# A fused adaLN block: who opens and who adds the eight partial groups of a feed-forward step

## The chip, the cores and the metric

The kernel runs on one core of a Trainium2 chip. The metric is the device time of one execution in microseconds.

## What is computed

The reference is one transformer-like block over 4096 tokens of width 512. Its first half (layer norm, a cumulative attention, a gated projection) is not touched. The second half is the feed-forward:

```python
h = _layernorm(x) * (1 + cb) + sb
gate_up = einsum('bsh,oh->bso', h, w_gu)      # w_gu: 2816 x 512, 4-bit values times scales
gate, up = gate_up[..., :1408], gate_up[..., 1408:]
y = einsum('bsi,hi->bsh', silu(gate) * up, w_down)
x = x + gb * (y / sqrt(mean(y * y) + 1e-6))
```

The scales of `w_gu` hold for groups of 128 input channels, so a product over 512 inputs is four group sums, each scaled by itself.

## The kernel before

The tokens are worked through in NB = 8 blocks of T = 512, features on the partitions. The function `ffn` is the second stage. A block has I_T = 11 steps j, one for each 128 hidden units. In a step TensorE computes GROUPS = 8 groups m: 0 to 3 are the four input groups of the gate, 4 to 7 those of the up half. Each is two matmuls (high and low part of the input) into one PSUM bank of `EV`. After every second group TensorE adds three matmuls of the down projection of step j - 2 (`down`), into four other banks. So a step has 28 matmuls of 128x512.

The banks: `ev_bank(j, m)` is m % 4, but m % 3 in the steps 2 to 5 (`R_STEPS`), where the fourth bank is `R`, used for the sums over channels. `before(j, m)` finds the group that had the bank last, and TensorE waits for its taker.

A group is taken out of its bank with its scale (`take`) into `A`, a float32 buffer with three slots of four tiles: the even groups by ScalarE, which opens a tile (L1445), the odd ones by VectorE, which scales and adds to the tile (L1621). So a step has four tiles, each the sum of two groups. GpSimd's `half` (L1525) adds tile 1 to tile 0 (gate) and tile 3 to tile 2 (up). ScalarE's `silu` (L1455) works on tile 0. `hidden` multiplies tile 0 by tile 2: on GpSimd (L1531) at the steps in `POOL_STEPS`, at the others on VectorE (L1628). ScalarE's `high` (L1451) rounds the product to float16 in `HH`, GpSimd's `low` (L1535) forms the rest, and both feed `down` (L1335) two steps later. ScalarE's first take of a step waits until `low` has left the slot (`slot_free`).

Each engine's order is written out by hand. Beside the takes, `beside` puts one instruction of the next block's norm and of the last block's output at fixed places; place 4j + i is the pair of groups i of step j. On VectorE these are: centring at places 9 to 12 (L1567), quarter reciprocals of the variance's root at 22 to 25 (L1573), the scale at 26 to 29 (L1585), the low part of the input (low_n, L1591) at 30 to 33, quarter reciprocals for the output at 34 to 37, its norm (L1598) at 38 to 41 and the result (L1613) at 40 to 43. GpSimd has nine additions at places 1 to 19 (L1505, L1514). The reductions on TensorE stand at places 8 (mean, L1313, which also waits for all takes of steps 0 and 1 in `sums_left`), 17 and 21.

Of the kernel before, what the change touches and what calls it, by code (L numbers as in the profile page):

```python
# [15 lines left out]
ALU = mybir.AluOpType  # L16
# [1122 lines left out]
def ffn(nc, v):  # L1139
# [7 lines left out]
    with ExitStack() as ctx:  # L1147
# [22 lines left out]
        EV = bank[0:4]  # L1170
# [10 lines left out]
        R_STEPS = range(2, 6)  # L1181

        def ev_bank(j, m):
            return m % (3 if j in R_STEPS else 4)
# [53 lines left out]

        POOL_STEPS = (1, 2, *range(5, I_T))

# [58 lines left out]
        def _(pe):  # L1299
# [6 lines left out]
            def sums_left(b):  # L1306

                pe.wait_ge(by_dve, DT * (I_T * b + R_STEPS.start))
                pe.wait_ge(by_act, DT * (I_T * b + R_STEPS.start))

# [30 lines left out]
            def iteration(b, s, prev, nxt):  # L1341
# [3 lines left out]
                for j in range(I_T):  # L1345
                    for m in range(GROUPS):
# [13 lines left out]
                        if last is None:  # L1360
                            n = b + 1 if nxt else b
                            bank_free(n, n, b if prev else 0)
                        elif not (j == 0 and last[0] and first(b)):

                            back, k = last
                            pe.wait_ge((by_act, by_dve)[k % 2], DT * (I_T * b + j - back) + k // 2 + 1)
                        which, g = m // DT, m % DT
# [17 lines left out]
            bank_free(NB - 1, NB - 1, NB - 1)  # L1385
            pe.wait_ge(by_dve, DT * I_T * NB)
            pe.wait_ge(by_act, DT * I_T * NB)
            for c in range(DT):
# [5 lines left out]
        def _(act):  # L1394
# [43 lines left out]
            def take(b, j, m):  # L1438
# [3 lines left out]
                if m == 0:  # L1442
                    slot_free(act, HH_low, b, j)
                t = which * I_T + j
                nc.scalar.activation(A[:, slot(j), 2 * which + g // 2, :], EV[ev_bank(j, m)][:], ACT.Copy,  # L1445
                                     scale=gu_s[:, t, g:g + 1]).then_inc(by_act, 1)
# [6 lines left out]
            def silu(b, j):  # L1453
                act.wait_ge(halves, 2 * (I_T * b + j) + 1)
                nc.scalar.activation(A[:, slot(j), 0, :], A[:, slot(j), 0, :], ACT.Silu).then_inc(gate_silu, 1)  # L1455
# [17 lines left out]
            def iteration(b, s, prev, nxt):  # L1473
                for j in range(I_T):
                    for m in range(0, GROUPS, 2):
                        beside(b, s, DT * j + m // 2, prev, nxt)
                        if m == GROUPS - 2:
                            if j:
                                high(b, j - 1)
                            elif prev:  # L1480
                                high(b - 1, I_T - 1)
                        take(b, j, m)
                    silu(b, j)
# [13 lines left out]
        def _(pool):  # L1497
# [23 lines left out]

            def half(b, j, which):
                pool.wait_ge(by_dve, DT * (I_T * b + j) + 2 * which + 2)
                a = A[:, slot(j), 2 * which, :]
                nc.gpsimd.tensor_tensor(a, a, A[:, slot(j), 2 * which + 1, :], ALU.add).then_inc(halves, 1)  # L1525

            def hidden(b, j):
                pool.wait_ge(gate_silu, I_T * b + j + 1)
                pool.wait_ge(halves, 2 * (I_T * b + j) + 2)
                a = A[:, slot(j), 0, :]  # L1530
# [14 lines left out]
            def iteration(b, s, prev, nxt):  # L1545
                for j in range(I_T):
                    if j in POOL_STEPS:
                        hidden(b, j - 1)
                    for i in range(DT):
                        if i == DT - 2:  # L1550
                            half(b, j, 0)
                        if i == DT - 1:
# [4 lines left out]
                        beside(b, DT * j + i, prev, nxt)  # L1557
                    half(b, j, 1)

# [4 lines left out]
        def _(dve):  # L1564
# [50 lines left out]
            def take(b, j, m):  # L1615

                which, g = m // DT, m % DT
                dve.wait_ge(group_done, GROUPS * (I_T * b + j) + m + 1)
                dve.wait_ge(by_act, DT * (I_T * b + j) + m // 2 + 1)
                a = A[:, slot(j), 2 * which + g // 2, :]  # L1620
                nc.vector.scalar_tensor_tensor(a, EV[ev_bank(j, m)][:], gu_s[:, which * I_T + j, g:g + 1], a,  # L1621
                                               ALU.mult, ALU.add).then_inc(by_dve, 1)

            def hidden(b, j):
                dve.wait_ge(gate_silu, I_T * b + j + 1)
                dve.wait_ge(halves, 2 * (I_T * b + j) + 2)
                a = A[:, slot(j), 0, :]
# [15 lines left out]
            def iteration(b, s, prev, nxt):  # L1643
                for j in range(I_T):
                    for m in range(1, GROUPS, 2):
                        beside(b, s, DT * j + m // 2, prev, nxt)
                        take(b, j, m)
# [50 lines left out]
```

## Time and profile before

| | |
|---|---|
| median of 3 runs | 2037.17 us (2035.51 to 2041.21) |
| span of the profiled execution, first to last instruction | 2036.9 us |
| TensorE busy | 1888.6 us (93%) |
| VectorE busy | 1382.7 us (68%) |
| GpSimd busy | 959.1 us (47%) |
| ScalarE busy | 921.8 us (45%) |
| granted TensorE clock, mean | 0.975 |

The profiled execution has no time of its own beside its span; the span is 0.3 us below the median of the runs. PE is TensorE, PEld its weight loads, DVE VectorE, ACT ScalarE, POOL GpSimd. Matmuls are pipelined: each is shown 0.38 us long, although the next begins before it ends. The first stage ends and the feed-forward begins at 1401 us.

### The profile page before, as it was taken

Reading aid. Unit: us, or ns where it says so; the run is one execution under the profiler, and the core shown is the slowest. Engines: PE = TensorE matmul, PEld = TensorE weight load, DVE = VectorE, ACT = ScalarE, POOL = GpSimd, SP = SyncE. Lnnn points to the kernel's source line nnn. Section 1 sums busy time; section 2 is a strip of 40 time slices with the busy share of each in tenths; the row PEclk is TensorE's granted clock in tenths of the full one; section 3 lists DMA queues with packets and bytes.
Section 4 is the critical chain, followed back from the end, with each engine's and each line's share of the span. In section 5 each row is a group of like instructions: output and inputs, shape, how many; then the busy total and the mean of one; then the engine's idle time right before and its main releaser. Section 6 shows DMA issues by size and latency. Waiting matters only on the chain. (4 is left out here: it accounts for less than half of the span.)

```text
span 2036.9 us, 25294 instructions
## 1 busy us (share of the span) xinstructions
PE 1888.6 (93%) x8376; PEld 826.3 (41%) x8376; DVE 1382.7 (68%) x1795; ACT 921.8 (45%) x1421; POOL 959.1 (47%) x680
## 2 busy tenths in 40 slices
PE   4638999999999999999999999998999999999996
PEld 1213444444444444444444444443443433433432
DVE  6996884884874866777678457245657768768756
ACT  4445334333423433523432421122776776776773
POOL 0553422421522521431441231213889889989974
PEclk7869999999999999999999999998999999999998
DMA  8223012012012012101101101313101011011011
GB/s 308 83 68 95 24 35 81 11 39 93 5 40 95 6 35 67 40 26 54 62 26 37 60 6 47 112 35 127 63 1 63 22 42 63 22 42 62 0 42 62
DMA packets 62147, 112.06 MB, mean 55 GB/s; under 512 B 4464, under 2 KB 20848, under 8 KB 61424
## 3 DMA queue, kind: packets, MB, share of 16 engines
q1 hardware_dynamic: 62064, 111.06, 16.3%
q8 instruction: 39, 0.64, 0.1%
q14 instruction: 44, 0.36, 0.1%
HBM read 80.11 MB, written 30.93 MB: 55 GB/s over the span
## 5 line engine op out<-in xcount | busy, mean ns | idle before, releaser
L532 PE MATMUL bank<-Y,wsw 128*128 128x512 f16 x3072 | 684.0, 379 | 8.7 <-DVE late L843 8.4
L786 POOL TENSOR_TENSOR late<-late 128x512 f16<-128x512 f32 x128 | 192.1, 1501 | 633.1 <-ACT late L661 633.0
L532 PEld LDWEIGHTS bank<-Y,wsw 128*128 128x128 f16 x3072 | 299.0, 98 | 376.6 <-DVE late L843 12.0
L1621 DVE SCALAR_TENSOR_TENSOR f_A<-bank,gu_s,f_A 128x512 f32<-128x512 f32 x352 | 260.7, 741 | 177.8 <-ACT f_A L1445 166.8
L509 PE MATMUL bank<-late,wout 128*128 128x512 f16 x1536 | 352.4, 379 | 3.6 <-POOL late L786 3.5
L1445 ACT ACTIVATE f_A<-bank,gu_s 128x512 f32<-128x512 f32 x352 | 241.6, 687 | 157.6 <-PE bank L1370 139.1
L487 PE MATMUL bank<-H,wqkv 128*128 128x512 f16 x1152 | 260.1, 387 | 37.0 <-DVE H L868 30.9
L1525 POOL TENSOR_TENSOR f_A<-f_A 128x512 f32<-128x512 f32 x176 | 253.9, 1443 | 72.9 <-DVE f_A L1621 72.4
L1335 PE MATMUL bank<-f_HH,f_down_hi 128*128 128x512 f16 x704 | 267.3, 382 | 20.2 <-POOL f_HH L1535 19.7
L843 DVE TENSOR_TENSOR late<-late,bank 128x512 f32<-128x512 f32 x128 | 87.7, 685 | 227.4 <-PE bank L532 206.8
L653 ACT ACTIVATE late<-bank 128x512 f32<-128x512 f32 x128 | 76.4, 597 | 350.1 <-PE bank L532 265.5
L509 PEld LDWEIGHTS bank<-late,wout 128*128 128x128 f16 x1536 | 149.6, 98 | 193.9 <-issue 19.2
L1370 PE MATMUL bank<-H,wqkv 128*128 128x512 f16 x704 | 187.3, 385 | 10.8 <-ACT f_A L1445 5.0
L661 ACT ACTIVATE late<-late 128x512 f16<-128x512 f32 x128 | 80.3, 627 | 252.9 <-DVE late L843 252.9
L1370 PE MATMUL bank<-f_H,wqkv 128*128 128x512 f16 x704 | 185.1, 379 | 7.3 <-DVE f_A L1621 4.1
L487 PEld LDWEIGHTS bank<-H,wqkv 128*128 128x128 f16 x1152 | 114.3, 100 | 187.2 <-issue 50.7
L839 DVE RECIPROCAL RD<-RD 128x512 f32<-128x512 f32 x25 | 83.7, 3348 | 74.9 <-ACT RD L584 74.9
L1335 PE MATMUL bank<-f_HH,f_down_lo 128*128 128x512 f16 x352 | 134.2, 381 | 0.0
L1335 PEld LDWEIGHTS bank<-f_HH,f_down_hi 128*128 128x128 f16 x704 | 69.0, 98 | 117.3 <-issue 39.4
L1535 POOL TENSOR_TENSOR f_HH<-f_A,f_HH 128x512 f16<-128x512 f32 x88 | 114.3, 1299 | 1.6 <-ACT f_HH L1451 1.5
L1370 PEld LDWEIGHTS bank<-H,wqkv 128*128 128x128 bf16 x704 | 66.5, 99 | 108.5 <-DVE f_A L1621 20.4
L1370 PEld LDWEIGHTS bank<-f_H,wqkv 128*128 128x128 bf16 x704 | 66.1, 98 | 101.5 <-DVE f_A L1621 18.4
(151 smaller groups left out, 2143.8 us busy)
## 6 DMA issues: line engine op xcount, KB each, us to landing
room<-packed SPq DMA_DIRECT2D x48, 176.0 KB, 2.4
X<-xT SPq DMA_DIRECT2D x8, 1024.0 KB, 6.0
h_scratch<-X SPq DMA_DIRECT2D x8, 1024.0 KB, 4.2
f_X<-x_scratch SPq DMA_DIRECT2D x8, 1024.0 KB, 5.5
f_N<-x_scratch SPq DMA_DIRECT2D x7, 1024.0 KB, 5.5
outT<-f_X SPq DMA_DIRECT2D x7, 1024.0 KB, 4.2
late<-xT SPq DMA_DIRECT2D x24, 256.0 KB, 2.9
HR<-h_scratch SPq DMA_DIRECT2D x24, 256.0 KB, 3.2
```

Of the source, the lines that this page charges most:

```text
L487: mm = nc.tensor.matmul(out[:], wqkv[:, pw, k, col:col + P], H[:, px, k, :], start=(k == 0 and pw == 0 and px == 0), stop=(k == DT - 1 and ...
L509: mm = nc.tensor.matmul(O_BANK[c][:], wout[:, pw, j, c * P:(c + 1) * P], UG[:, j % 2, px, :], start=(j == 0 and pw == 0 and px == 0), stop ...
L532: mm = nc.tensor.matmul(out[:], wsw[:, pw, k, col:col + P], Y[:, px, k, :], start=(k == 0 and pw == 0 and px == 0), stop=(k == DT - 1 and ...
L786: nc.gpsimd.tensor_tensor(UG[:, j % 2, 1, :], G, UG[:, j % 2, 0, :], ALU.subtract).then_inc(UG_low, 1)
L839: nc.vector.reciprocal(DEV[kind], DEV[kind]).then_inc(recip[kind], 1)
L843: nc.vector.tensor_tensor(dst, a, b_, ALU.mult).then_inc(done, 1)
L1335: mm = nc.tensor.matmul(O[c][:], w[:, col:col + P], HH[:, slot(j), part, :], start=(j == 0 and w is down_hi and part == 0), stop=(j == I_T ...
L1370: mm = nc.tensor.matmul(EV[ev_bank(j, m)][:], values[:, col:col + P], H[s][:, part, g, :], start=part == 0, stop=part == 1)
L1445: nc.scalar.activation(A[:, slot(j), 2 * which + g // 2, :], EV[ev_bank(j, m)][:], ACT.Copy, scale=gu_s[:, t, g:g + 1]).then_inc(by_act, 1)
L1525: nc.gpsimd.tensor_tensor(a, a, A[:, slot(j), 2 * which + 1, :], ALU.add).then_inc(halves, 1)
L1535: nc.gpsimd.tensor_tensor(HH[:, slot(j), 1, :], A[:, slot(j), 0, :], HH[:, slot(j), 0, :], ALU.subtract).then_inc(HH_low, 1)
L1621: nc.vector.scalar_tensor_tensor(a, EV[ev_bank(j, m)][:], gu_s[:, which * I_T + j, g:g + 1], a, ALU.mult, ALU.add).then_inc(by_dve, 1)
```

## The change

Every step now has three partial tiles. ScalarE opens them with groups 0, 2 and 4. VectorE adds groups 1 and 3 as before and then 5, 6 and 7, all three into the up tile, which so is complete without a `half`; only the gate's half stays on GpSimd. The SiLU waits for that half, and `hidden` for VectorE's last take. `POOL_STEPS` becomes all steps but 0, so of a block's products only the one done in the next block's step 0 stays on VectorE. VectorE's take waits for the group before it in the tile, by ScalarE's or its own semaphore. In VectorE's order take 6 stands ahead of the beside work of its pair, and take 7 behind it.

```diff
--- before.py
+++ after.py
@@ -1180,6 +1180,12 @@
         GROUPS = 2 * DT
         R_STEPS = range(2, 6)
 
+
+        BY_ACT = (0, 2, 4)
+        BY_DVE = (1, 3, 5, 6, 7)
+        PART = (0, 0, 1, 1, 2, 2, 2, 2)
+        NA, ND = len(BY_ACT), len(BY_DVE)
+
         def ev_bank(j, m):
             return m % (3 if j in R_STEPS else 4)
 
@@ -1236,7 +1242,7 @@
         INVERT_Y, NORM_Y, RESULT = 34, 38, 40
 
 
-        POOL_STEPS = (1, 2, *range(5, I_T))
+        POOL_STEPS = range(1, I_T)
 
         def now(place, start, step=1):
 
@@ -1305,8 +1311,8 @@
 
             def sums_left(b):
 
-                pe.wait_ge(by_dve, DT * (I_T * b + R_STEPS.start))
-                pe.wait_ge(by_act, DT * (I_T * b + R_STEPS.start))
+                pe.wait_ge(by_dve, ND * (I_T * b + R_STEPS.start))
+                pe.wait_ge(by_act, NA * (I_T * b + R_STEPS.start))
 
             def mean(b):
                 pe.wait_ge(x_sum, NSUM * b)
@@ -1363,7 +1369,10 @@
                         elif not (j == 0 and last[0] and first(b)):
 
                             back, k = last
-                            pe.wait_ge((by_act, by_dve)[k % 2], DT * (I_T * b + j - back) + k // 2 + 1)
+                            if k in BY_ACT:
+                                pe.wait_ge(by_act, NA * (I_T * b + j - back) + BY_ACT.index(k) + 1)
+                            else:
+                                pe.wait_ge(by_dve, ND * (I_T * b + j - back) + BY_DVE.index(k) + 1)
                         which, g = m // DT, m % DT
                         col = (g * 2 * I_T + which * I_T + j) * P
                         for part in range(2):
@@ -1383,8 +1392,8 @@
                 for c in range(DT):
                     down(NB - 1, j, c)
             bank_free(NB - 1, NB - 1, NB - 1)
-            pe.wait_ge(by_dve, DT * I_T * NB)
-            pe.wait_ge(by_act, DT * I_T * NB)
+            pe.wait_ge(by_dve, ND * I_T * NB)
+            pe.wait_ge(by_act, NA * I_T * NB)
             for c in range(DT):
                 pe.wait_ge(y_squared, DT * (NB - 1) + c + 1)
                 mm = nc.tensor.matmul(R[:], ones[:], SQY[:, c, :], start=c == 0, stop=c == DT - 1)
@@ -1442,7 +1451,7 @@
                 if m == 0:
                     slot_free(act, HH_low, b, j)
                 t = which * I_T + j
-                nc.scalar.activation(A[:, slot(j), 2 * which + g // 2, :], EV[ev_bank(j, m)][:], ACT.Copy,
+                nc.scalar.activation(A[:, slot(j), PART[m], :], EV[ev_bank(j, m)][:], ACT.Copy,
                                      scale=gu_s[:, t, g:g + 1]).then_inc(by_act, 1)
 
             def high(b, j):
@@ -1451,7 +1460,7 @@
                 nc.scalar.activation(HH[:, slot(j), 0, :], A[:, slot(j), 0, :], ACT.Copy).then_inc(HH_high, 1)
 
             def silu(b, j):
-                act.wait_ge(halves, 2 * (I_T * b + j) + 1)
+                act.wait_ge(halves, I_T * b + j + 1)
                 nc.scalar.activation(A[:, slot(j), 0, :], A[:, slot(j), 0, :], ACT.Silu).then_inc(gate_silu, 1)
 
             def beside(b, s, place, prev, nxt):
@@ -1479,7 +1488,8 @@
                                 high(b, j - 1)
                             elif prev:
                                 high(b - 1, I_T - 1)
-                        take(b, j, m)
+                        if m in BY_ACT:
+                            take(b, j, m)
                     silu(b, j)
 
             blocks(act, iteration)
@@ -1519,14 +1529,14 @@
             def add_y(b, n):
                 add(b, n, SQY, RSY, y_squared, y_sum, y_red, b)
 
-            def half(b, j, which):
-                pool.wait_ge(by_dve, DT * (I_T * b + j) + 2 * which + 2)
-                a = A[:, slot(j), 2 * which, :]
-                nc.gpsimd.tensor_tensor(a, a, A[:, slot(j), 2 * which + 1, :], ALU.add).then_inc(halves, 1)
+            def half(b, j):
+                pool.wait_ge(by_dve, ND * (I_T * b + j) + 2)
+                a = A[:, slot(j), 0, :]
+                nc.gpsimd.tensor_tensor(a, a, A[:, slot(j), 1, :], ALU.add).then_inc(halves, 1)
 
             def hidden(b, j):
                 pool.wait_ge(gate_silu, I_T * b + j + 1)
-                pool.wait_ge(halves, 2 * (I_T * b + j) + 2)
+                pool.wait_ge(by_dve, ND * (I_T * b + j + 1))
                 a = A[:, slot(j), 0, :]
                 nc.gpsimd.tensor_tensor(a, a, A[:, slot(j), 2, :], ALU.mult).then_inc(hid_ready, 1)
 
@@ -1548,14 +1558,13 @@
                         hidden(b, j - 1)
                     for i in range(DT):
                         if i == DT - 2:
-                            half(b, j, 0)
+                            half(b, j)
                         if i == DT - 1:
                             if j:
                                 low(b, j - 1)
                             elif prev:
                                 low(b - 1, I_T - 1)
                         beside(b, DT * j + i, prev, nxt)
-                    half(b, j, 1)
 
             blocks(pool, iteration)
             low(NB - 1, I_T - 1)
@@ -1616,14 +1625,17 @@
 
                 which, g = m // DT, m % DT
                 dve.wait_ge(group_done, GROUPS * (I_T * b + j) + m + 1)
-                dve.wait_ge(by_act, DT * (I_T * b + j) + m // 2 + 1)
-                a = A[:, slot(j), 2 * which + g // 2, :]
+                if m - 1 in BY_ACT:
+                    dve.wait_ge(by_act, NA * (I_T * b + j) + BY_ACT.index(m - 1) + 1)
+                else:
+                    dve.wait_ge(by_dve, ND * (I_T * b + j) + BY_DVE.index(m - 1) + 1)
+                a = A[:, slot(j), PART[m], :]
                 nc.vector.scalar_tensor_tensor(a, EV[ev_bank(j, m)][:], gu_s[:, which * I_T + j, g:g + 1], a,
                                                ALU.mult, ALU.add).then_inc(by_dve, 1)
 
             def hidden(b, j):
                 dve.wait_ge(gate_silu, I_T * b + j + 1)
-                dve.wait_ge(halves, 2 * (I_T * b + j) + 2)
+                dve.wait_ge(by_dve, ND * (I_T * b + j + 1))
                 a = A[:, slot(j), 0, :]
                 nc.vector.tensor_tensor(a, a, A[:, slot(j), 2, :], ALU.mult).then_inc(hid_ready, 1)
 
@@ -1643,6 +1655,8 @@
             def iteration(b, s, prev, nxt):
                 for j in range(I_T):
                     for m in range(1, GROUPS, 2):
+                        if m - 1 in BY_DVE:
+                            take(b, j, m - 1)
                         beside(b, s, DT * j + m // 2, prev, nxt)
                         take(b, j, m)
                         if m == 3:
```

## Rows read from the trace of the kernel before

**Rows 1.** Windows: us, busy time (and count) of each engine, granted clock, DMA.
```profile
1401.00:2020.60 619.60, 575.65 (x2507) 240.90 (x2506) 434.44 (x580) 423.63 (x678) 527.67 (x391) 0.99 0.13 44
...
1646.32:1722.78 76.46, 71.50 (x314) 30.05 (x314) 56.30 (x75) 54.06 (x88) 67.92 (x51) 1.00 0.13 42
```

**Rows 2.** The same view, steps 7, 9 and 10 of that block.
```profile
1681.97:1688.67 6.70, 6.21 (x29) 2.67 (x28) 6.43 (x9) 6.07 (x11) 6.62 (x5) 1.00 0.00 0
...
1695.28:1701.32 6.04, 6.04 (x29) 2.73 (x28) 5.94 (x9) 3.78 (x7) 5.27 (x5) 1.00 0.27 104
1701.32:1708.56 7.24, 6.55 (x29) 2.50 (x28) 7.24 (x9) 3.60 (x6) 5.27 (x4) 1.00 0.00 0
```

**Rows 3.** Timeline of TensorE: start, length, what, idle before and its releaser.
```profile
1646.32 1.12 PE L1313 MATMUL bank<-f_RS,ones 128*128 128x512 f32 x2 [0.57 <-DVE f_A L1621]
...
1653.92 0.60 PE L1370 MATMUL bank<-f_H,wqkv 128*128 128x512 f16 x2 [0.43 <-ACT f_A L1445]
...
1662.12 0.38 PE L1335 MATMUL bank<-f_HH,f_down_hi 128*128 128x512 f16 x1 [0.43 <-POOL f_HH L1535]
...
1676.35 0.60 PE L1370 MATMUL bank<-f_H,wqkv 128*128 128x512 f16 x2 [0.30 <-DVE f_A L1621]
...
1683.49 0.38 PE L1335 MATMUL bank<-f_HH,f_down_hi 128*128 128x512 f16 x1 [0.49 <-POOL f_HH L1535]
...
1707.47 0.60 PE L1370 MATMUL bank<-f_H,wqkv 128*128 128x512 f16 x2 [0.60 <-DVE f_A L1621]
...
1710.85 0.38 PE L1335 MATMUL bank<-f_HH,f_down_hi 128*128 128x512 f16 x1 [1.26 <-POOL f_HH L1535]
```

**Rows 4.** Timeline of VectorE in the same block.
```profile
1673.36 0.94 DVE L1573 RECIPROCAL f_RV<-f_RV 128x128 f32<-128x128 f32 x1
...
1677.82 0.75 DVE L1621 SCALAR_TENSOR_TENSOR f_A<-bank,gu_s,f_A 128x512 f32<-128x512 f32 x1 [0.66 <-ACT f_A L1445]
...
1684.16 0.75 DVE L1621 SCALAR_TENSOR_TENSOR f_A<-bank,gu_s,f_A 128x512 f32<-128x512 f32 x1 [0.27 <-ACT f_A L1445]
...
1702.72 1.75 DVE L1613 TENSOR_TENSOR f_X<-f_X,f_Y 128x512 f32<-128x512 f32 x1
...
1706.68 0.74 DVE L1621 SCALAR_TENSOR_TENSOR f_A<-bank,gu_s,f_A 128x512 f32<-128x512 f32 x1
1707.34 0.68 DVE L1613 TENSOR_TENSOR f_X<-f_X,f_Y 128x512 f32<-128x512 f32 x1
```

**Rows 5.** Timeline of GpSimd in the same block.
```profile
1659.60 1.27 POOL L1505 TENSOR_TENSOR f_RSY<-f_RSY,f_SQY 128x512 f32<-128x512 f32 x1
1660.83 1.14 POOL L1535 TENSOR_TENSOR f_HH<-f_A,f_HH 128x512 f16<-128x512 f32 x1
...
1707.49 1.65 POOL L1525 TENSOR_TENSOR f_A<-f_A 128x512 f32<-128x512 f32 x1 [1.90 <-DVE f_A L1621]
1709.10 1.61 POOL L1535 TENSOR_TENSOR f_HH<-f_A,f_HH 128x512 f16<-128x512 f32 x1
```

**Rows 6.** The page's part 5: busy us, mean ns, idle before and its releaser.
```profile
L1445 ACT ACTIVATE f_A<-bank,gu_s 128x512 f32<-128x512 f32 x352 | 241.6, 687 | 157.6 <-PE bank L1370 139.1
```

**Rows 7.** Timeline of VectorE in the first stage.
```profile
1204.00 0.52 DVE L957 SCALAR_TENSOR_TENSOR room<-room 128x352 f32<-128x352 f32 x1
1204.56 0.34 DVE L961 TENSOR_SCALAR room<-room 128x352 f32<-128x352 int32 x1
```

**Rows 8.** Groups by line on VectorE, 1673.3 to 1711.2.
```profile
L1613 DVE TENSOR_TENSOR f_X<-f_X,f_Y 128x512 f32<-128x512 f32 x4 | 4.2, 1050 | 0.0
L1591 DVE SCALAR_TENSOR_TENSOR H<-f_N,mod,H 128x512 f16<-128x512 f32 x4 | 3.9, 978 | 0.0
...
L1598 DVE SCALAR_TENSOR_TENSOR f_Y<-f_Y,mod,f_RY 128x512 f32<-128x512 f32 x4 | 3.7, 929 | 0.0
L1585 DVE SCALAR_TENSOR_TENSOR f_N<-f_N,mod,f_RV 128x512 f32<-128x512 f32 x4 | 3.6, 892 | 0.0
```

**Rows 9.** Windows, near the end of the last block.
```profile
2013.40:2017.60 4.20, 4.10 (x12) 1.53 (x13) 0.69 (x1) 0.63 (x1) 2.33 (x2) 0.59 0.65 243
```

## The prediction

> **What bounds the kernel now.** I read the page's busy shares first, then the window of the whole second stage, then one repeating block step by step, and then each engine's timeline through that block. The second stage (the feed-forward) runs from 1401 to 2020.6. TensorE is its main engine, GpSimd is busy 527.7 of its 619.6 us, VectorE 434.4, ScalarE 423.6 [rows 1]. So GpSimd, which the change relieves, is the busiest helper on average. The blocks repeat: the one from 1646.32 to 1722.78 takes 76.46 us [rows 1], and blocks 1 to 6 all look like it.
>
> How much of a block is TensorE's own work? Step 9 runs without any stall: 28 matmuls in 6.04 us, 0.216 us each [rows 2]. A block has 308 such matmuls (66.4 us) and three reductions of some 0.92 us in float32 (2.8 us). That leaves 7.3 us of stalls per block, and all that the change can win or lose is in them. A matmul is shown 0.38 us long but its successor may start after 0.216, so a stall is the idle time shown plus 0.16.
>
> The larger stalls of the block [rows 3]: the mean's reduction at step 2 waits 0.73 for VectorE's last sum; at the starts of steps 3 and 6 a bank is given back late (0.59 and 0.46); the down projection waits for GpSimd's `low` at steps 4, 7 and 0 (0.59, 0.65 and 1.42); in step 10 a wait for VectorE costs 0.76. Together 5.2 of the 7.3; the rest are gaps of the same kinds. GpSimd is the named releaser of half of it, so the change looks right. But what made GpSimd late? From 1673.36 VectorE works nearly back to back: its beside work begins with the variance's reciprocals, and a quarter reciprocal or a scale stands ahead of each take. Until the take of group 3 in step 10 (1706.68, ending at 1707.42) it waits three times, 0.66, 0.27 and once more as long as that [rows 4]. That take releases the gate half on GpSimd at 1707.49, this the `low` at 1709.10, and this TensorE at 1710.85, the 1.42 us stall [rows 3, 5]. In steps 7 and 10 VectorE is busy 6.43 of 6.70 and 7.24 of 7.24 us [rows 2]. From step 5 to step 10, VectorE sets the pace of the block, and GpSimd only passes it on. In steps 7 and 8 both are full: GpSimd is busy 6.62 of 6.70 us [rows 2].
>
> **The change part by part**, for a middle block.
>
> *ScalarE* loses the take of group 6, 0.69 us [rows 6], and had room already (423.6 of 619.6 us busy). TensorE's and VectorE's waits on that take turn into waits on VectorE's.
>
> *GpSimd* loses the up half in every step (an addition of two tiles takes 1.27 us, or 1.65 when it collides [rows 5]), and gains the product in steps 3 and 4, some 1.27 us each, where VectorE had it. It is then far from full. At step 4 the stall comes from an addition (1659.60) and the `low` (1660.83, ending as the down projection starts) queued behind a half that VectorE's product had slowed [rows 3, 5]. With the product in GpSimd's own queue ahead of it and the half clear, `low` ends some 0.5 us earlier. Gain 0.6, and I allow 0.1 more at the variance, whose sum comes earlier: -0.7. If `low` came no earlier, this would be 0. The moved product is hidden: GpSimd does it at the start of a step and ScalarE's `high` comes only after take 4. The last product of a block stays on VectorE.
>
> *VectorE, the path.* Each step gets one more take, group 6, and groups 5, 6 and 7 now form a chain into one tile. Between 1673.36 and the take of group 3 in step 10 lie five new ones (steps 5 to 9). A take followed by independent work costs 0.66 start to start (1706.68 to 1707.34) [rows 4]. Take 6 must wait for the end of take 5. I take 0.75 + 0.04 from a decoding instruction that starts 0.04 after its 0.52 us predecessor ends [rows 7]. Five of them: 3.9 us. Against this stand the three waits, 1.2 us, which they fill, and less collision with GpSimd. Where both read two tiles of SBUF, both take longer: low_n 0.978, norm 0.929 and scale 0.892 on average against 0.74 of a take, the same operation, and the result 1.050 against 0.68 [rows 4, 8]. The excess is 4 x (0.24 + 0.19 + 0.15 + 0.37) = 3.8 us per block. GpSimd will have three instructions in a step instead of four, so about a fifth less, 0.8, comes back. Net: 3.9 - 1.2 - 0.8 = +1.9 us. The bounds: +2.7 if no collision goes, -1.1 if all do. In TensorE's timeline I expect it so: the wait at the start of step 6 grows from 0.46 to about 1.2, since take 6, a reciprocal and take 7 of step 5 stand ahead of the bank; step 7's down wait goes; step 10's two VectorE waits grow to some 0.9 each, and the 1.4 at step 0 remains, moved later.
>
> The Trainium skill (SBUF — State Buffer, section "SBUF: two separate sides") says that the port pair shared by VectorE and GpSimd is an exclusive lock, the later one blocked until the first ends. These rows show less: an excess of 0.15 to 0.37 on average, and one result of 1.75 us against 0.68 that comes near to it [rows 4, 8]. By the rule each of the 16 instructions would lose half a GpSimd instruction for the three quarters of the time that GpSimd is busy, some 7.7 us, and a fifth of that is 1.5, not 0.8: the sum would be +1.2.
>
> *Steps 2 to 5.* Where three banks serve, the next group 1 (and the mean's reduction) needs take 7. Before: take 6 by ScalarE (0.69 [rows 6]), then take 7. After: take 6 by VectorE (0.75), then take 7, +0.06 to 0.1 at four places: +0.3. It could be less than nothing only where ScalarE's `high` delayed take 6, at step 3; there the centring instruction on VectorE takes its place.
>
> *Elsewhere.* No DMA is added or moved; the loads and stores of SP's queue wait on things long done. The first stage is untouched.
>
> **The sum.** A middle block: 1.9 - 0.7 + 0.3 = +1.5, six of them +9. Block 0 has no output work but a fifth take beside the mixer's sums, where the mean waits for VectorE: I take +1. Block 7 has only the output work: two new takes before group 3 of step 10 (+1.6), of which the missing half at the very end gives little back, since the last down projection runs behind the one before it: +1. In all +11. The profiled execution's span is 2036.9 and the median of the runs 2037.2, with 0.3 us around the span at most: **2048 us**.
>
> **Rivals.** *(1) Gains and losses cancel.* If half of the collisions go (1.9 us), a block gains 0.7, adds 0.3 and nets 3.9 - 1.2 - 1.9 = +0.8: +0.4 per block, +4 in all, 2041. For it: in steps 8 to 10 GpSimd will be idle between its three instructions; against it: its halves are released by VectorE's own takes and so fall just on the beside work. Chance 0.26. *(2) Faster.* All collisions go, -1.1, and the half and `low` ahead of step 0 shrink from 1.65 and 1.61 to 1.27 and 1.16, -0.8: with -0.7 and +0.3 that is -2.3 a block, -14, and some +1 at the ends: 2024. It decides from the point where 2.7 us or more of the 3.8 go. Against it: in step 10 norm, result and two more stand around each half. Chance 0.10. *(3) The clock falls.* After TensorE's wait for the last block's `low`, ahead of 2013.5, the granted clock was 0.59 over 4.2 us, so half speed (1.2 GHz) for most of it [rows 9], and the 12 matmuls that began in it would have needed 2.6 us at full speed, so 1.6 us were lost. The 1.42 us stall at step 0 did not do it. If three stalls of 0.9 to 1.4 within 6 us did so in each middle block, 6 x 1.6 = 10 us come on top: 2058. Chance 0.07. The forecast itself has 0.57.
>
> **The numbers.** Below about 0.3% (6 us) no measurement of this kernel tells a change from none. Slower takes the forecast and rival 3: 0.64; same is rival 1: 0.26; faster is rival 2: 0.10. The forecast's own range is 2044 to 2055 (a block from +1.0 to +2.3, the upper bound of the collisions). The range for 8 in 10 leaves out rival 2 and rival 3 and takes in rival 1: 2036 to 2056.
>
> **What would show it.** Right, if in the new profile VectorE has no wait between the first reciprocal and take 3 of step 10, that stretch grows from 34.1 to some 36 us, step 4's wait for `low` is gone, and a block takes about 78.0 us against 76.46. TensorE's waits on GpSimd should fall below 1.5 us a block beside step 0's, and those on VectorE in steps 6 and 10 double. Wrong, if the beside instructions come down to 0.74 and 0.68 (then rival 2), if blocks shorten although VectorE is full (then the reading of VectorE as the pacer fails), or if the granted clock leaves 1.00 inside the blocks.

## The result and the profile after

The changed kernel takes 2054.32 us (median of 4 runs, 2054.13 to 2054.76), against 2037.56 us of the kernel before on the same chip: 1.0080 times as long, with an interval of 1.0066 to 1.0094. The forecast was 2048 us, in a range of 2036 to 2056. So it is slower, as forecast, but by 16.8 us where the sum said 11. The profiled execution has a span of 2052.9 us against 2036.9. Below, take 3 is short for VectorE's take of group 3.

The page of the kernel after, part 1 and four groups of part 5 (busy us, mean ns, idle before and its releaser):

```profile
PE 1887.9 (92%) x8376; PEld 821.4 (40%) x8376; DVE 1437.6 (70%) x1867; ACT 868.7 (42%) x1333; POOL 846.0 (41%) x608
...
L1633 DVE SCALAR_TENSOR_TENSOR f_A<-bank,gu_s,f_A 128x512 f32<-128x512 f32 x440 | 324.2, 738 | 139.5 <-ACT f_A L1454 120.2
...
L1454 ACT ACTIVATE f_A<-bank,gu_s 128x512 f32<-128x512 f32 x264 | 181.1, 686 | 173.8 <-PE bank L1379 154.3
...
L1535 POOL TENSOR_TENSOR f_A<-f_A 128x512 f32<-128x512 f32 x88 | 127.3, 1447 | 150.6 <-DVE f_A L1633 150.6
...
L1541 POOL TENSOR_TENSOR f_A<-f_A 128x512 f32<-128x512 f32 x80 | 110.2, 1377 | 57.4 <-DVE f_A L1633 57.0
```

The change did what it says: 440 takes on VectorE (L1633), 264 on ScalarE (L1454), 88 halves (L1535), 80 products on GpSimd (L1541). GpSimd lost 113 us of work and waits now: all of the idle time ahead of its halves ends with VectorE's takes.

The same block as before lasts 78.85 us, from the mean's reduction at 1652.65 to the next at 1731.50. The block before lasts 76.48: its next mean begins at 1722.80, 0.02 behind the end of the window in [rows 1].

```profile
1722.80 1.12 PE L1313 MATMUL bank<-f_RS,ones 128*128 128x512 f32 x2 [0.57 <-DVE f_A L1621]
```

The changed block's window is the next row (busy us of TensorE, its weight loads, VectorE, ScalarE and GpSimd; granted clock; DMA share and GB/s):

```profile
1652.65:1731.50 78.85, 71.69 (x314) 29.61 (x315) 63.28 (x84) 47.51 (x76) 53.67 (x42) 1.00 0.12 41
```

The granted clock is 1.00 in it. TensorE's timeline in this block, the rows with its larger waits, from the mean's reduction on (start, length, then the idle time before it and its releaser):

```profile
1652.65 1.12 PE L1319 MATMUL bank<-f_RS,ones 128*128 128x512 f32 x2 [1.03 <-DVE f_A L1633]
...
1660.98 0.61 PE L1379 MATMUL bank<-f_H,wqkv 128*128 128x512 f16 x2 [0.65 <-DVE f_A L1633]
...
1683.08 0.61 PE L1379 MATMUL bank<-f_H,wqkv 128*128 128x512 f16 x2 [0.82 <-DVE f_A L1633]
...
1696.44 0.38 PE L1341 MATMUL bank<-f_HH,f_down_hi 128*128 128x512 f16 x1 [0.67 <-POOL f_HH L1545]
...
1703.12 0.38 PE L1341 MATMUL bank<-f_HH,f_down_hi 128*128 128x512 f16 x1 [0.41 <-POOL f_HH L1545]
...
1710.06 0.38 PE L1341 MATMUL bank<-f_HH,f_down_hi 128*128 128x512 f16 x1 [0.71 <-POOL f_HH L1545]
...
1714.18 0.61 PE L1379 MATMUL bank<-f_H,wqkv 128*128 128x512 f16 x2 [1.31 <-DVE f_A L1633]
...
1716.10 0.60 PE L1379 MATMUL bank<-f_H,wqkv 128*128 128x512 f16 x2 [0.24 <-DVE f_A L1633]
...
1719.03 0.38 PE L1341 MATMUL bank<-f_HH,f_down_hi 128*128 128x512 f16 x1 [0.81 <-POOL f_HH L1545]
```

Against [rows 3]: the down waits of steps 4 and 7 are gone; the wait early in step 3 is 0.81 instead of 0.59, and the one at the start of step 6 is 0.98 instead of 0.46 (0.16 is added to each idle time shown, as in the prediction); steps 9 and 10 have new waits for `low` of 0.57 and 0.87; step 10 waits for VectorE for 1.47 and 0.40 instead of 0.76; step 0's wait fell from 1.42 to 0.97; and the mean's grew from 0.73 to 1.19. Step 8's wait for `low` grew from 0.57 to 0.83; before the change it was this row, which the prediction's list leaves out:

```profile
1690.10 0.38 PE L1335 MATMUL bank<-f_HH,f_down_hi 128*128 128x512 f16 x1 [0.41 <-POOL f_HH L1535]
```

Where a block's 2.37 us come from is plain once it is cut at two instructions of VectorE, the first quarter reciprocal of the variance and the take of group 3 in step 10:

| stretch | before | after | difference | forecast |
|---|---|---|---|---|
| mean to first reciprocal | 1646.32 to 1673.36: 27.04 | 1652.65 to 1679.30: 26.65 | -0.39 | -0.7 + 0.3 |
| first reciprocal to end of take 3 | to 1707.42: 34.06 | to 1716.05: 36.75 | +2.69 | +1.9 |
| take 3 to the next mean | to 1722.80: 15.38 | to 1731.50: 15.45 | +0.07 | 0 |

The middle line is where the sum was too small. Over the whole: the first mean comes 1.2 us later (0.55 of it because the feed-forward begins later, behind a first stage that the change doesn't touch), block 0 adds 0.4 to that, the five periods after it 2.26 to 2.71 each (12.2), and the stretch from the last mean to the end 2.2: 16.0 us.

### The profile page after: what moved, and what is told of

Its sections match the earlier page's. It is cut to its first block and busy times, and to the rows that moved or that the text cites. A ratio compares the mean times of both kernels' runs of the same rounds, so it can differ in the third digit from the quotient of the medians.

```text
span 2052.9 us, 25432 instructions
## 1 busy us (share of the span) xinstructions
PE 1887.9 (92%) x8376; PEld 821.4 (40%) x8376; DVE 1437.6 (70%) x1867; ACT 868.7 (42%) x1333; POOL 846.0 (41%) x608
## 5 line engine op out<-in xcount | busy, mean ns | idle before, releaser
L1633 DVE SCALAR_TENSOR_TENSOR f_A<-bank,gu_s,f_A 128x512 f32<-128x512 f32 x440 | 324.2, 738 | 139.5 <-ACT f_A L1454 120.2
L1454 ACT ACTIVATE f_A<-bank,gu_s 128x512 f32<-128x512 f32 x264 | 181.1, 686 | 173.8 <-PE bank L1379 154.3
L1535 POOL TENSOR_TENSOR f_A<-f_A 128x512 f32<-128x512 f32 x88 | 127.3, 1447 | 150.6 <-DVE f_A L1633 150.6
L1541 POOL TENSOR_TENSOR f_A<-f_A 128x512 f32<-128x512 f32 x80 | 110.2, 1377 | 57.4 <-DVE f_A L1633 57.0
```

The costliest lines, as they stand in the source:

```text
L1454: nc.scalar.activation(A[:, slot(j), PART[m], :], EV[ev_bank(j, m)][:], ACT.Copy, scale=gu_s[:, t, g:g + 1]).then_inc(by_act, 1)
L1535: nc.gpsimd.tensor_tensor(a, a, A[:, slot(j), 1, :], ALU.add).then_inc(halves, 1)
L1541: nc.gpsimd.tensor_tensor(a, a, A[:, slot(j), 2, :], ALU.mult).then_inc(hid_ready, 1)
```

## Why less work on GpSimd did not shorten VectorE's instructions

VectorE's timeline of the kernel after, at both ends of that middle stretch and at three of its instructions:

```profile
1679.30 0.94 DVE L1582 RECIPROCAL f_RV<-f_RV 128x128 f32<-128x128 f32 x1
...
1698.75 1.09 DVE L1600 SCALAR_TENSOR_TENSOR H<-f_N,mod,H 128x512 f16<-128x512 f32 x1
...
1706.92 0.74 DVE L1607 SCALAR_TENSOR_TENSOR f_Y<-f_Y,mod,f_RY 128x512 f32<-128x512 f32 x1
...
1711.71 1.75 DVE L1622 TENSOR_TENSOR f_X<-f_X,f_Y 128x512 f32<-128x512 f32 x1
...
1714.71 0.68 DVE L1622 TENSOR_TENSOR f_X<-f_X,f_Y 128x512 f32<-128x512 f32 x1
1715.31 0.74 DVE L1633 SCALAR_TENSOR_TENSOR f_A<-bank,gu_s,f_A 128x512 f32<-128x512 f32 x1
```

GpSimd's timeline of the same kernel, the instructions beside them and the last two before step 0's wait:

```profile
1697.59 1.71 POOL L1541 TENSOR_TENSOR f_A<-f_A 128x512 f32<-128x512 f32 x1 [1.29 <-DVE f_A L1633]
...
1707.09 1.71 POOL L1535 TENSOR_TENSOR f_A<-f_A 128x512 f32<-128x512 f32 x1 [1.58 <-DVE f_A L1633]
...
1711.20 1.71 POOL L1541 TENSOR_TENSOR f_A<-f_A 128x512 f32<-128x512 f32 x1 [1.29 <-DVE f_A L1633]
1716.12 1.65 POOL L1535 TENSOR_TENSOR f_A<-f_A 128x512 f32<-128x512 f32 x1 [3.21 <-DVE f_A L1633]
1717.73 1.15 POOL L1545 TENSOR_TENSOR f_HH<-f_A,f_HH 128x512 f16<-128x512 f32 x1
```

The product at 1711.20 ends at 1712.91. The result that began 0.51 behind it ends at 1713.46, which is 0.55 after the product, where the result alone takes 0.68. The low part at 1698.75 ends at 1699.84, 0.54 after the product of 1697.59, where it takes 0.74 alone. So the later of the two does not run slower beside the other; it waits for it. It goes the other way round too: the half at 1707.09 began 0.17 behind a norm that ends at 1707.66, and ends 1.14 later, its own 1.27 less 0.13. I went through both engines' timelines of the middle blocks (1480 to 1960, 96 of VectorE's instructions that read two tiles of SBUF: scale, `low_n`, norm and result), before and after. In both kernels every one of them that began inside an instruction of GpSimd (its last 0.13 us left out) ended 0.54 to 0.56 us after GpSimd's (one 0.61), whatever its own length. The ones that began first kept 0.74 or 0.68.

| kernel | began inside an instruction of GpSimd | lost by them against 0.74 or 0.68 | per block |
|---|---|---|---|
| before | 69 of 96 | 22.8 us | 3.8 us |
| after | 42 of 96 | 25.5 us | 4.2 us |

Is it this that the middle stretch is made of? In the blocks 3 to 6 it lasts 34.05 to 34.07 us before, of which 3.36 to 3.39 are such losses, and 36.74 to 36.75 after, with 3.56 or 3.57. Without the losses it is 30.7 in every one of these blocks before and 33.2 in every one after. So the five new takes, less the idle time that they fill, cost 2.5 us, and the losses did not fall.

GpSimd's four instructions a step ran nearly back to back before, and VectorE's mostly met the rest of one (0.33 us lost by a meeting). After, fewer meet, but each waits nearly twice as long (0.61): half and product are released by VectorE's own takes 3 and 7, so they and the `low` behind them start just ahead of, or just behind, the instruction that follows the take. The groups by line on VectorE, 1679.3 to 1720.8, against [rows 8]:

```profile
L1622 DVE TENSOR_TENSOR f_X<-f_X,f_Y 128x512 f32<-128x512 f32 x4 | 4.5, 1132 | 0.0
L1600 DVE SCALAR_TENSOR_TENSOR H<-f_N,mod,H 128x512 f16<-128x512 f32 x4 | 4.0, 996 | 0.0
...
L1594 DVE SCALAR_TENSOR_TENSOR f_N<-f_N,mod,f_RV 128x512 f32<-128x512 f32 x4 | 3.7, 930 | 0.0
L1607 DVE SCALAR_TENSOR_TENSOR f_Y<-f_Y,mod,f_RY 128x512 f32<-128x512 f32 x4 | 3.6, 912 | 0.0
```

The prediction held averages like these against a rule of the Trainium skill (SBUF — State Buffer, section "SBUF: two separate sides": the shared port pair is an exclusive lock, held by whoever starts first) and found that the rows show less. That was misread. Met one by one, the instructions of these two kernels agree with the rule but for the 0.1 to 0.2 us by which they overlap; the averages are small because in the kernel before those that met began late in GpSimd's instruction, and because after the change more than half come first or meet nobody. What was wrong in both sums, with the rule and without it, is the step from there: to let the loss fall with GpSimd's number of instructions, as if they met by chance.

## The experiments

The theory: VectorE sets the pace from step 5 to step 10, its fifth take is the cost, and GpSimd passes the delay on. The rival: GpSimd's chain, or TensorE's other waits, hold the time by themselves. Each kernel ran beside the kernel before on the same chip; the ratio is against that one.

### The fifth take made tiny

Group 6's take works on 8 of 512 columns, so the rest of group 6 is missing from the up sum.

```diff
+                w = 8 if m == 6 else T
-                nc.vector.scalar_tensor_tensor(a, EV[ev_bank(j, m)][:], ..., a,
+                nc.vector.scalar_tensor_tensor(a[:, 0:w], EV[ev_bank(j, m)][:, 0:w], ..., a[:, 0:w],
```

> The changed kernel, but VectorE's new take of group 6 handles 8 of 512 columns (the rest of that group is left out of the sum); order, waits and banks stay. If VectorE sets the pace from step 5 to step 10 (my theory), the stretch from the first reciprocal to the take of group 3 in step 10 falls from 36.75 us by nearly five takes, to some 33.5 to 34, a block from 78.9 to 75 to 76, and the kernel to 2027 to 2036. If the loss came from the new order and its waits (the chain of takes 5, 6, 7 behind a bank) or from GpSimd, only the starts of steps shorten: a block loses 1 us or less and the time is 2047 or more.

Measured: 2032.79 us against 2039.24, ratio 0.9971 (0.9962 to 0.9981). The middle stretch falls from 36.75 to 34.21 us, a little less than expected, and the block from 78.85 to 76.03. In TensorE's timeline the wait for `low` at step 4 comes back in part, and the one at the start of step 6 is 0.87 instead of 0.98:

```profile
1660.10 0.38 PE L1341 MATMUL bank<-f_HH,f_down_hi 128*128 128x512 f16 x1 [0.36 <-POOL f_HH L1545]
...
1674.60 0.60 PE L1379 MATMUL bank<-f_H,wqkv 128*128 128x512 f16 x2 [0.71 <-DVE f_A L1634]
```

The length of one of VectorE's instructions in each step is worth some 22 us, more than the whole change costs. With that away the rest of the change is a gain of 0.3%: the fifth take is the cause, and the rest pays a little of it back.

### The moved product, put back

```diff
-        POOL_STEPS = range(1, I_T)
+        POOL_STEPS = (1, 2, *range(5, I_T))
```

> The changed kernel with the products of steps 2 and 3 back on VectorE, as before the change. If moving the product is what ended step 4's wait for GpSimd's low (0.6 us per block), the wait returns and the kernel is 3 to 5 us slower than the changed one (2057 to 2059). If the missing up half alone ended it, the time stays at 2054, within 1.

`hidden` does a step's product in the step after it: the products of steps 2 and 3, as the expectation has them, are VectorE's work in steps 3 and 4.

Measured: 2059.02 us, ratio 1.0100 (1.0082 to 1.0118). With these products on VectorE again, step 4's wait is back:

```profile
1671.72 0.38 PE L1341 MATMUL bank<-f_HH,f_down_hi 128*128 128x512 f16 x1 [0.39 <-POOL f_HH L1545]
```

The other waits from step 5 on are those of the changed kernel. The time is 4.7 us longer by the medians and 4.1 by the ratios, whose intervals overlap. The traces, 4.5 us apart, say where: 1.4 are there at block 0's mean in step 2, where the edit has changed nothing yet, 1.2 come in the rest of block 0, and each of the five periods behind it is 0.3 to 0.4 longer (27.02 us instead of 26.65 from the mean to the first reciprocal of the block shown). So the product's move alone is worth some 0.4 us in a middle block. That the time fell into the expected 2057 to 2059 is in part luck.

### The moved product alone

The same line, in the kernel before.

> The kernel before with only the product of steps 2 and 3 moved to GpSimd. GpSimd has no idle time to give in steps 3 and 4 there, so I expect its low to come later: slower by 0 to 6 us (2037 to 2043). If the collision with VectorE's product is what costs most at step 4, it is faster by up to 4.

Measured: 2044.87 us, ratio 1.0031 (1.0017 to 1.0044), at the upper end of what was expected. Here the move costs, 0.9 us in each middle block. TensorE's timeline, step 4's `low` and the variance's reduction:

```profile
1664.69 0.38 PE L1335 MATMUL bank<-f_HH,f_down_hi 128*128 128x512 f16 x1 [0.61 <-POOL f_HH L1535]
...
1673.29 1.10 PE L1317 MATMUL bank<-f_RS,ones 128*128 128x512 f32 x2 [0.42 <-POOL f_RS L1505]
```

Without the room that the missing up halves leave, GpSimd has two instructions more among the additions of steps 2 to 4. The same edit makes a middle block of the one kernel 0.4 us shorter and of the other 0.9 longer.

### The mean's two waits in the other order

Of the 0.46 us by which the mean's wait grew, the longer chain explains less than half: take 7 ends 0.44 before the mean starts, and ended 0.14 before it in the kernel before. The mean waits for takes of both engines, and the wait for VectorE stands first. Either wait's value is worked out from the block's number, and the second may be worked out only once the first wait is over.

```diff
-                pe.wait_ge(by_dve, ND * (I_T * b + R_STEPS.start))
                 pe.wait_ge(by_act, NA * (I_T * b + R_STEPS.start))
+                pe.wait_ge(by_dve, ND * (I_T * b + R_STEPS.start))
```

> The changed kernel with the two waits ahead of the mean's reduction in the other order: ScalarE's, long fulfilled, first, VectorE's second. The reduction now starts 0.44 us after take 7 in the blocks of the loop and 0.16 in blocks 1 and 2, whose numbers are constants. If the cause is the value of the second wait, worked out only after the first wait has ended, the reduction starts some 0.28 us earlier in the four blocks 3 to 6 and idle time before it falls from 1.03 to some 0.75; the kernel gains about 1 us. If not, 1.03 stays.

Measured: 2053.79 us (2 runs), ratio 1.0075 (1.0051 to 1.0099), which by its time can't be told from the changed kernel. The trace can: the mean's wait is 0.72 instead of 1.03 in the blocks whose number is in a register.

```profile
1652.01 1.12 PE L1319 MATMUL bank<-f_RS,ones 128*128 128x512 f32 x2 [0.72 <-DVE f_A L1633]
```

The span is 1.9 us shorter, 1.2 of it in the periods with such a mean. In blocks 1 and 2, whose number is a constant, it was 0.75 with the first order, too (0.80 with the second). Before the change both waits had the same number, four takes a step by either engine, and afterwards two different ones: the price of the second value is 0.3 us. That the value comes from a register is what sets these blocks apart, but how the engine works a value out no run shows: this step is only argued.

### The results of a block's output, taken out of step 10

If VectorE is too full in step 10, its four result additions may go to where it waits: the places 0, 2, 4 and 6 of the next block, in its steps 0 and 1. First in the changed kernel, then in the kernel before.

```diff
+                due, c = now(place, 0, 2)
+                if prev and not (isinstance(b, int) and b == 1) and due:
+                    result(b - 2, c)
...
-                        ... (prev, b - 1, RESULT, result)):
+                        ... (prev and not nxt, b - 1, RESULT, result)):
```

> The changed kernel, with the four result additions of a block (L1622, 1.13 us on average) moved on VectorE from places 40 to 43 to places 0, 2, 4 and 6 of the next block, where VectorE waits between its takes. If VectorE sets the pace through step 10, two results (1.67 and 0.60 start to start) leave the stretch ahead of the take of group 3 in step 10 and it falls from 36.75 to some 34.5; steps 0 and 1 have less room than they take back, so a block gains 1.5 to 2.3 us and the kernel is at 2038 to 2044. If GpSimd or the banks set the pace, it stays at 2052 or more.

Measured: 2047.56 us against 2038.34, ratio 1.0047 (1.0031 to 1.0064). The middle stretch is 34.8 us, 1.9 less, and both waits for VectorE in step 10 are gone. But the mean's wait grows by 0.8, which the expectation (2038 to 2044) had left out, and the block gains only 1.3:

```profile
1649.91 1.12 PE L1319 MATMUL bank<-f_RS,ones 128*128 128x512 f32 x2 [1.84 <-DVE f_A L1633]
```

> The kernel before, with the same move of the results. If VectorE set the pace of step 10 there too, the stretch falls from 34.06 to some 31.8, step 10's waits for VectorE and the 1.42 us wait at step 0 shrink, and the kernel is at 2022 to 2028. If the full GpSimd, with four instructions a step, set it, the move gives under 4 us (2033 or more).

Measured: 2031.17 us, ratio 0.9965 (0.9951 to 0.9979). The stretch falls from 34.06 to 31.8, the idle time ahead of the mean grows from 0.57 to 1.50. The move is worth 7 us in either kernel, about half of what was expected, and for the same reason: in step 1 the results and GpSimd's instructions hold one another up, take 7 comes later, and the mean waits for it. In the changed kernel a result at 1723.09 lasts 1.67 behind an addition of GpSimd's; in the kernel before GpSimd's product at 1714.73 lasts 1.84 beside a result, and ScalarE's `high` and take 6 come behind it.

### Three tiles only in steps 2 to 4

By the profile, the fifth take costs where VectorE is full (steps 5 to 10), and GpSimd's relief pays at step 4. So three tiles in the steps 2, 3 and 4, four in the others, with all products but step 0's on GpSimd and the mean's waits swapped.

```diff
+        THREE = (2, 3, 4)
+        BY_ACT = [(0, 2, 4) if j in THREE else (0, 2, 4, 6) for j in range(I_T)]
+        BY_DVE = [(1, 3, 5, 6, 7) if j in THREE else (1, 3, 5, 7) for j in range(I_T)]
+        PART = [(0, 0, 1, 1, 2, 2, 2, 2) if j in THREE else (0, 0, 1, 1, 2, 2, 3, 3) for j in range(I_T)]
...
```

> The change in steps 2, 3 and 4 alone (three tiles, no up half there), four tiles elsewhere as before, every product but the last on GpSimd, and the two waits ahead of the mean swapped as in the run before. From step 5 on the old work of VectorE comes back: the stretch is 34.06 again, step 4's wait for low stays gone. A block takes 75.8 to 76.2 instead of 76.46 and the kernel 2032 to 2035. If the loss is not in steps 5 to 10, it stays above 2040.

Measured: 2035.71 us (10 runs), ratio 0.9986 (0.9976 to 0.9996). The middle stretch is 34.02 us and the block 76.03, both as expected; the time lies 0.7 us above the expected 2032 to 2035. TensorE's timeline has no wait for `low` before step 7, and step 0's is the one of before:

```profile
1677.07 0.61 PE L1396 MATMUL bank<-f_H,wqkv 128*128 128x512 f16 x2 [0.35 <-DVE f_A L1649]
1684.16 0.38 PE L1358 MATMUL bank<-f_HH,f_down_hi 128*128 128x512 f16 x1 [0.45 <-POOL f_HH L1562]
...
1711.53 0.38 PE L1358 MATMUL bank<-f_HH,f_down_hi 128*128 128x512 f16 x1 [1.27 <-POOL f_HH L1562]
```

Taking the three tiles out of eight of the eleven steps gave back 0.94% (19 us), all of the change's cost. The gain that is left is 0.14%, less than the 0.3% of the prediction's limit; its interval leaves out 1 only because there are ten runs.

> Both: the change in steps 2 to 4 alone, and the results moved to the next block's first two steps. If the two effects lie in different steps, as I think, they add: 2018 to 2024. If GpSimd becomes the pacer from step 6 on, most of the second is lost: 2030.

With the late results on top: 2029.02 us, ratio 0.9957 (0.9943 to 0.9972). The time lies at the 2030 that the expectation gave to GpSimd as the pacer, but the trace says otherwise: the middle stretch is 31.75 us, as with the late results alone. The two gains add (2.6 and 7 us of the 9.3), and the miss is again the mean's, with 1.49 us of idle time.

### GpSimd's half left out

This asks how much of the changed kernel's time is GpSimd's own. The half is not done, so gate groups 2 and 3 are missing from the sum; the SiLU waits for VectorE's take 3 itself.

```diff
-                act.wait_ge(halves, I_T * b + j + 1)
+                act.wait_ge(by_dve, ND * (I_T * b + j) + 2)
...
-                        if i == DT - 2:
-                            half(b, j)
```

> The changed kernel without GpSimd's half: the SiLU waits for VectorE's take of group 3 and works on the first gate tile alone (the sum of the gate's groups 2 and 3 is left out). GpSimd has then two instructions a step, product and low, and low is not queued behind a half. If VectorE sets the pace, the waits for low vanish (3.3 us a block in the changed kernel) but the stretch up to the take of group 3 in step 10 stays at 35.5 to 36.8 us and a block at 77 to 78.5: 2042 to 2051. If GpSimd's lateness set the pace, a block loses all of 3.3 us and the kernel is at 2031 or less. It shows also whether VectorE's beside instructions collide less when GpSimd has a third less to do: 0.93, 1.00, 0.91 and 1.13 us are to beat.

Measured: 2039.61 us (10 runs) against 2038.52, ratio 1.0002 (0.9993 to 1.0012). All of TensorE's waits for `low` go, and waits for VectorE take their places:

```profile
1695.82 0.61 PE L1379 MATMUL bank<-f_H,wqkv 128*128 128x512 f16 x2 [0.42 <-DVE f_A L1631]
...
1705.09 0.61 PE L1379 MATMUL bank<-f_H,wqkv 128*128 128x512 f16 x2 [1.31 <-DVE f_A L1631]
1707.97 0.60 PE L1379 MATMUL bank<-f_H,wqkv 128*128 128x512 f16 x2 [1.20 <-DVE f_A L1631]
```

The time lies below the 2042 to 2051 of VectorE as the only pacer and above the 2031 of GpSimd as the pacer. In the block shown the middle stretch is 36.1 us (1671.79 to 1707.92), as expected: with a third of GpSimd's instructions gone it shrinks by 0.6 only, which is what the meetings lose less (2.95 against 3.56 us in it). So it is in the blocks 1, 3 and 5. But in the blocks 2, 4 and 6 it is 34.5 to 34.7, 2.3 shorter, and the expectation of 35.5 to 36.8 fails there. The place is in step 10, where a norm of VectorE's, GpSimd's product and a result follow closely, first in block 3, then in block 4:

```profile
1702.12 1.70 POOL L1541 TENSOR_TENSOR f_A<-f_A 128x512 f32<-128x512 f32 x1 [1.83 <-DVE f_A L1631]
1702.62 1.75 DVE L1620 TENSOR_TENSOR f_X<-f_X,f_Y 128x512 f32<-128x512 f32 x1
...
1779.86 2.31 POOL L1541 TENSOR_TENSOR f_A<-f_A 128x512 f32<-128x512 f32 x1 [1.83 <-DVE f_A L1631]
1780.36 0.68 DVE L1620 TENSOR_TENSOR f_X<-f_X,f_Y 128x512 f32<-128x512 f32 x1
```

Both times the product begins inside the norm and the result 0.50 behind the product. In block 3 the product ends 1.12 after the norm, and the result waits for it. In block 4 the result goes first, keeps its 0.68, and the product ends 1.13 after the result. The losses in the stretch are then 1.27 us. Without the losses the stretch is 33.2 in the blocks 3 to 6 alike, as in the changed kernel: it is VectorE's own work and what it loses by meetings, with the half or without. Why the order differs from block to block stays open.

The whole fell by 15.5 us of span: 9.1 in the six periods, 2.8 up to the first mean and 3.7 from the last. Of the 8.2 in the five periods behind block 0, 6.5 lie in the middle stretch, 1.1 behind it and 0.7 ahead of it. So GpSimd's half does cost time, and mostly not as a link between take 3 and TensorE's down projection, but by the meetings that it makes for VectorE.

### Three tiles in steps 2 to 4, and the results split

Results 0 and 1 go to the last two places of step 10, results 2 and 3 to the first and third place of the next block, so that none stands in step 1.

```diff
+                if prev and nxt and place >= 42:
+                    result(b - 1, place - 42)
+                if prev and not (isinstance(b, int) and b == 1) and place in (0, 2):
+                    result(b - 2, 2 + place // 2)
...
```

> The change in steps 2 to 4 alone, with two of the four results at the end of step 10 (places 42 and 43) and two at places 0 and 2 of the next block. The stretch is as short as with all results moved (31.8), but only half of the collisions fall into steps 0 and 1, so the mean's wait, which grew from 0.57 to 1.49 us there, goes back to 0.6 to 1.0: 2024 to 2028, against 2029 of the run with all results moved. If the mean's wait stays at 1.5, 2029 or more.

Measured: 2027.37 us (5 runs) against 2038.52, ratio 0.9939 (0.9926 to 0.9953). It is faster than both kernels. TensorE's timeline: the first and the last row are two means, 74.33 us apart, the shortest of the five periods behind block 0 (up to 75.8), and the one between is all that is left of the waits around step 10:

```profile
1642.67 1.12 PE L1336 MATMUL bank<-f_RS,ones 128*128 128x512 f32 x2 [0.56 <-DVE f_A L1649]
...
1704.91 0.38 PE L1358 MATMUL bank<-f_HH,f_down_hi 128*128 128x512 f16 x1 [0.40 <-POOL f_HH L1562]
1717.00 1.12 PE L1336 MATMUL bank<-f_RS,ones 128*128 128x512 f32 x2 [0.56 <-DVE f_A L1649]
```

## Why the prediction was right, and where its size was off

**VectorE paces steps 5 to 10: right.** Between the first reciprocal and take 3 of step 10 it has no idle time above 0.14 us, and making one take tiny gives the time back. The step 6 wait grew to 0.98 (forecast 1.2), step 10's to 1.47 and 0.40 (forecast 0.9 each).

**Five new takes at 3.9 us, less 1.2 of idle time filled: right within 0.3.** The two terms give +2.7, and without the losses by meetings the stretch grew by 2.5 (30.7 to 33.2). The new takes added 3.3 us of busy time, 0.67 each, and idle time fell from 1.3 to 0.5. With the losses (3.4 before, 3.6 after) it is the +2.7 measured.

**"About a fifth less, 0.8, comes back": the term that failed.** Nothing came back; it was the stated upper bound, "+2.7 if no collision goes", that happened. Per block this is 0.8 of the 0.9 us between forecast (+1.5) and result (+2.4), and with six blocks 4.8 of the 5.8 us between 11 and 16.8. The step that failed is the one from fewer instructions to less loss: what was measured is 3.8 us a block before and 4.2 after.

**Step 4's `low` and the variance, -0.7: right in the trace.** The wait of 0.59 at step 4 is gone, and so is 0.10 at the variance. The prediction put it down to the product's move and the missing half together, and so it is: the move alone is worth 0.4 us a block in the changed kernel, and a loss of 0.9 without the missing half.

**Three banks and the mean, +0.3: right in sum with the term before** (-0.39 measured, -0.4 forecast, although the mean's own part falls into the last stretch of the table). That the mean would pay 0.3 us for the second wait's value was not seen; it was made up for by a half and a `low` ahead of step 0 that took 1.65 and 1.15 instead of 1.65 and 1.61 [rows 5].

**Waits on GpSimd below 1.5 us a block beside step 0's: wrong.** They are 2.3, and were 2.2 before: the prediction's list left out the 0.57 of step 8 and the 0.34 in step 3. The reading that GpSimd "only passes it on" leaves out that its instructions hold up VectorE's: without its half the changed kernel is 15 us shorter, for the most part by smaller losses on VectorE.

**The ends, +1 and +1:** the first mean and block 0 cost 1.6 for the first, 0.55 of it from ahead of the feed-forward; the 2.2 from the last mean to the end hold the rest of block 6, some 2.3, so nothing is left for block 7.

**The rivals.** The first (cancel, 2041) needed half of the losses by meetings to go, the second (faster, 2024) 2.7 us of them; they rose by 0.4 instead. The third (clock) did not happen: the block's window has a granted clock of 1.00, in spite of waits of 0.87, 1.47, 0.40 and 0.97 within 9 us.

## What to carry to other kernels

Ask which engine a relief reaches. GpSimd was the busiest helper over the stage, but VectorE's takes released it at the steps that set the end; work moved from one engine to another pays only in the steps where the first is late and the second has room (here steps 2 to 4), and a table by step says which. And before counting on fewer collisions between two engines, look at when the other's instructions are released: if they are released by the waiting engine itself, as here, they can keep on meeting it.

## What the runs showed of the hardware

- An instruction of VectorE that reads two SBUF tiles and one of GpSimd follow one another: the later ends 0.54 to 0.56 us (VectorE's, of 0.68 or 0.74 alone; one 0.61) or 1.12 to 1.14 us (a GpSimd addition or product of 1.27 by itself) after the earlier. Where GpSimd's instruction already waits behind one of VectorE's and VectorE's next one comes, either can go first: without the half, GpSimd's product did in three middle blocks and VectorE's result in the three others. Takes, which read one operand from PSUM, and the quarter reciprocals keep their 0.65 to 0.75 or 0.94 us inside an instruction of GpSimd.
- TensorE idled 1.03 us ahead of the mean with a second wait for another number, worked out from the block's number in a register, behind the long one, and 0.72 with that wait first. Where the block's number was a constant it was 0.75 and 0.80. Before the change, with two waits for the same number, the mean began 0.14 us after take 7; with the second number behind, 0.44.
- A take of VectorE that needs VectorE's own take before it starts 0.79 us after that take's start, and an instruction that needs nothing new 0.66 after: so a pair of takes is shown as 1.53 or 1.40 us.
